# Four-block gated cross-attention kernel: L1's attention in two passes over the batches with split fp32r weights, L3's scores in two halves

## What is computed

```
h   = layernorm(x);   xq = fp8(clip(h / in_scale))      
q, qx = xq @ wq, xq @ wqx  (2 heads a group);  k, v = xq @ wk, xq @ wv  (1 head a group)
kx, vx = ctx @ w_kv_x                                         # in fp32
q, k, qx, kx = layernorm of each head over its 128 features, times weight, plus bias
out = softmax(q k / sqrt(128)) v   and   softmax(qx kx / sqrt(128)) vx      # 4 heads a group in all
x  += gate * proj_scale * (fp8(out / smooth) @ wproj)         # contraction over 2 x 16 heads x 128
```

## Time and profile before

| | us |
|---|---|
| median of 3 runs (2734.95 to 2738.09) | 2735.35 |
| the profiled execution's own time | 2733.31 |
| its span in the trace | 2731.5 |
| L1 attention, 423.6 to 1521 | 1097.4 |
| L3 attention, from its first score at 2462.4 to about 2695 | 233 |

### The profile page before, as it was taken

The page is one execution under the profiler, slowest core; times in us unless marked ns, Lnnn a source line. Parts: engine busy times, 40 slices in busy tenths (PEclk is TensorE's granted clock), DMA queues, the critical chain, the costliest instruction groups (busy, mean ns, idle before and its releaser), DMA issues. The chain is left out here.

```text
span 2731.5 us, 50212 instructions
## 1 busy us (share of the span) xinstructions
PE 2318.3 (85%) x16586; PEld 1983.6 (73%) x16586; DVE 1921.9 (70%) x4961; ACT 1281.8 (47%) x3929; POOL 1194.8 (44%) x2657
## 2 busy tenths in 40 slices
PE   5879991799999999999999599997999994657776
PEld 2368881688888888888888488886888883335555
DVE  5855555688888888888888477776455555975665
ACT  2123321566666666666665233332344442435663
POOL 5800002577777777777777111110344442222222
PEclk9989995999999999999999699998899997768998
DMA  3100004000000000000000300001000000000000
GB/s 130 58 1 1 1 1 187 5 3 3 3 3 3 3 3 3 3 3 4 5 2 1 105 24 24 24 18 47 12 7 7 7 4 0 1 32 28 21 21 32
DMA packets 28880, 57.66 MB, mean 21 GB/s; under 512 B 4816, under 2 KB 22544, under 8 KB 27152
## 3 DMA queue, kind: packets, MB, share of 16 engines
q1 hardware_dynamic: 28624, 54.45, 6.0%
HBM read 52.34 MB, written 2.10 MB: 20 GB/s over the span
## 5 line engine op out<-in xcount | busy, mean ns | idle before, releaser
L1096 PE MATMUL bank<-l_w,l_xq 128*128 128x128 f32 (+1 forms) x2048 | 359.0, 329 | 9.9 <-DVE l_xq L1260 7.1
L1096 PEld LDWEIGHTS bank<-l_w,l_xq 128*128 128x128 f32 x2048 | 300.7, 192 | 31.2 <-DVE l_xq L1260 7.5
L1339 DVE TENSOR_SCALAR xn_T<-xn_T,l_tiny 128x128 f32<-128x128 f32 x768 | 297.1, 453 | 8.4 <-POOL l_tiny L1380 8.3
L1209 ACT ACTIVATE l_qt<-bank,l_head_b,l_head_w 128x256 f32<-128x256 f32 x256 | 144.4, 564 | 288.8 <-PE bank L1141 288.8
L1268 DVE BATCH_NORM_STATS2 l_st<-xn_T 128x6 f32<-128x128 f32 x768 | 212.4, 279 | 13.3 <-ACT l_v L1201 13.0
L788 PE MATMUL bank<-m_xr,m_wgr 128*128 128x512 f32 x864 | 211.1, 394 | 9.2 <-POOL m_wgr L848 9.2
L1388 POOL TENSOR_TENSOR l_pr<-l_pr,l_rowsum 128x512 f32<-128x512 f32 x128 | 134.3, 1049 | 158.5 <-DVE l_rowsum L1334 158.5
L214 POOL TENSOR_TENSOR ln_rstd<-ln_tmp,neg_half 128x16 f32<-128x16 f32 x8 | 23.3, 2910 | 382.0 <-DVE ln_tmp L152 382.0
L788 PEld LDWEIGHTS bank<-m_xr,m_wgr 128*128 128x128 f32 x864 | 159.0, 190 | 39.5 <-issue 9.2
L1183 ACT ACTIVATE l_pr<-bank,l_negmax 128x128 f32<-128x128 f32 x512 | 182.0, 384 | 1.6 <-DVE l_negmax L1347 1.6
L1370 POOL TENSOR_TENSOR l_tiny<-l_tiny,l_consts 128x6 f32<-128x6 f32 x128 | 177.7, 1388 | 10.0
(11 more groups left out here) (318 smaller groups left out, 6267.6 us busy)
## 6 DMA issues: line engine op xcount, KB each, us to landing
l_w<-in_l_w SPq DMA_DIRECT2D x1, 6144.0 KB, 18.1
m_unsplit<-in_m_w SPq DMA_DIRECT2D x14, 384.0 KB, 3.2
m_wg<-in_m_gu SPq DMA_DIRECT2D x18, 256.0 KB, 2.7
l2f_w<-in_l_w SPq DMA_DIRECT2D x3, 1024.0 KB, 6.9
m_wd<-in_m_down SPq DMA_DIRECT2D x18, 128.0 KB, 2.5
x_resident<-in_x SPq DMA_DIRECT2D x4, 512.0 KB, 5.5
l_ctxT<-in_ctxT SPq DMA_DIRECT2D x1, 2048.0 KB, 7.2
l_toep<-in_l_toep SPq DMA_DIRECT2D x16, 128.0 KB, 2.0
```

Of the source, the lines that this page charges most:

```text
L1096: e.matmul(bank[:, to:to + width], XQ[:, v, k, :], W[:, k, g, at:at + width], start=k == 0, stop=k == KT - 1)
L1209: e.activation(tok(QT[:, n % 2, 3 * x:3 * x + 2, :]), ps[:, 0:2 * P], ACT.Identity, bias=head_b[:, 2 * x:2 * x + 1], scale=head_w[:, 2 * x ...
L1339: r = e.tensor_scalar(RAW[:, n % 4, m, :], RAW[:, n % 4, m, :], tiny[:, n % 2, 0, m:m + 1], tiny[:, n % 2, 6, m:m + 1], ALU.subtract, ALU. ...
```

## The change

*L1 attention.* Two passes over the 16 batches, groups 0 to 3 in the first and 4 to 7 in the second: n = 4 q + j, q from 0 to 31, batch q % 16. Weights of only four groups are kept (WR, WXR, WPR), each in two fp32r parts, high and low. They come one group at a time through a room of two slots of 1 MB, which also holds L0's context before; its first two loads are issued when L0's attention ends, the others inside the loop (LOADS). A group is prepared in numbered steps (FILL_PRE, FILL_POST, FILL_OUT): DVE sums each head's weight columns (`fill_means`), POOL subtracts the means in place (`fill_centre`), ACT scales and writes the high part (`fill_high`), DVE and POOL the low parts (`fill_low`, `fill_cross_low`); the output weights likewise on ACT and POOL. Since centred weights give heads whose mean is zero, the norm needs only the sum of squares: ACT squares all six heads in one instruction, DVE reduces them, POOL's statistics have six operations, and DVE's norm is one multiply. Projections are fp32r products with both parts (W) or three of four (context). Exponents lose the accumulator; DVE sums the probabilities (`sum_probs`). The last rounding subtraction of the output goes to POOL. Inputs are scaled on POOL (`affine`), rounded into XS (bf16), stored to HBM in pass one and fetched in pass two, and copied to a doubled XQ by ACT. The residual is added once in each pass. The layernorm ahead no longer counts again.

*L3 attention.* Scores, maxima and exponents go in two halves of four heads; turns and values come one step later; all values of a half batch are one block, two half batches share one bank. DVE makes the fourth copy of turned blocks instead of the first, and adds the result to X itself.

Other hunks only rename semaphores so that stages share them, and lay out the weights by group on the host. The diff, cut to its core:

```diff
@@ project
-                        for k in range(KT):
-                            e.matmul(bank[:, to:to + width], XQ[:, v, k, :], W[:, k, g, at:at + width], start=k == 0, stop=k == KT - 1)
+                        for k in range(KT):
+                            for part in range(2):
+                                e.matmul(bank[:, to:to + width], XQ[:, q % 2, v, k, :], WR[:, j, part, k, at:at + width],
+                                         start=k == 0 and part == 0, stop=k == KT - 1 and part == 1)
                 for k in range(KT):
-                    r = e.matmul(pcross[:, 2 * P:4 * P], CX[:, k, :], WX[:, k, g, :], start=k == 0, stop=k == KT - 1)
+                    for m, (a, c) in enumerate(((0, 0), (0, 1), (1, 0))):
+                        r = e.matmul(pcross[:, 2 * P:4 * P], CXR[:, q % 2, a, k, :], WXR[:, j, c, k, :],
+                                     start=k == 0 and m == 0, stop=k == KT - 1 and m == 2)
@@ tables of the loop
+            FILL_PRE = {0: 0, 1: 1, 2: 5, 3: 7, 4: 62, 5: 63, 6: 71, 7: 72}
+            FILL_POST = {0: 3, 1: 4, 2: 6, 3: 8, 4: 70, 5: 71, 6: 73, 7: 74}
+            FILL_OUT = {0: 9, 1: 10, 2: 11, 3: 12, 4: 76, 5: 77, 6: 78, 7: 79}
+            LOADS = (4, 5, 7, 9, 11, 13, 71, 72, 74, 75)
+            END = N + 18
@@ scalar: raw, square, fills
-                    e.copy(tok(RAW[:, n % 4, 3 * m:3 * m + 3, :]), bank[:, 0:3 * P])
-                    r = e.copy(V[:, n % G, m, :], bank[:, 3 * P:4 * P])
+                    r = e.copy(tok(RAW[:, n % 6, 4 * m:4 * m + 4, :]), bank[:, :])
+            def square(e, n):
+                e.wait_ge(*s_raw(n + 1))
+                if n >= 1:
+                    e.wait_ge(*s_ss(n))
+                e.activation(SQ[:, :, :].rearrange("p (a h) d -> p a h d", a=2), heads(n), ACT.Square).then_inc(s_sq.sem, 1)
+            def fill_high(e, f):
...
+                for v, at, width in SPAN:
+                    for k in range(KT):
+                        e.activation(WR[:, slot, 0, k, at:at + width], W[:, k, at:at + width], ACT.Copy, scale=full_scale[:, v, k:k + 1])
+                e.copy(WXR[:, slot, 0, :, :].rearrange("p k c -> p (k c)"), unsplit(f)[:, 6 * D:8 * D]).then_inc(s_whi.sem, 1)
@@ vector
+                    n = s - 17
+                    if 0 <= n < N and n % J == J - 1:
...
+                    out = 0 <= s - 15 < N
+                    if out:
+                        smooth_out(e, s - 15)
+                    if 0 <= s - 10 < N:
+                        sum_squares(e, s - 10)
+                    if out:
+                        round_out(e, s - 15, 0)
...
+                    summed = sum_probs(e, s - 13) if 0 <= s - 13 < N else None
+                    if out:
+                        round_out(e, s - 15, 1)
+                    if summed:
+                        e.wait_ge(*summed)
+                        e.reciprocal(rowsum[:, (s - 13) % 2, :], rowsum[:, (s - 13) % 2, :]).then_inc(s_inv.sem, 1)
+                    if out:
+                        round_out(e, s - 15, 2)
+                    if s >= 4 and s // J - 1 < B:
+                        quantise_x(e, s // J - 1, s % J)
+                    if out:
+                        round_out(e, s - 15, 3)
+                    if 0 <= s - 11 < N:
+                        norm(e, s - 11)
+                    if 0 <= s - 12 < N:
+                        maximum(e, s - 12)
...
+                    if s in pre:
+                        fill_means(e, pre[s])
+                    if s in post:
+                        fill_low(e, post[s])
+            def norm(e, n):
+                e.wait_ge(*s_rstd(n + 1))
+                rs = tiny[:, n % 2, 3, :].rearrange("p (a h) -> p a h", a=2)
+                e.tensor_tensor(heads(n), heads(n), bc(rs, 3, P), ALU.mult).then_inc(s_norm.sem, 1)
@@ gpsimd
+                    if s in pre:
+                        fill_centre(e, pre[s])
...
+                    n = s - 15
+                    if 0 <= n < N:
+                        e.wait_ge(*s_to(n + 1))
+                        if n >= 2:
+                            e.wait_ge(*s_outp(n - 1))
+                        e.tensor_tensor(tok(CAT[:, n % 2, :, :]), YO[:, n % 2, :], EO[:, :], ALU.subtract).then_inc(s_cat.sem, 1)
                     if 0 <= s - 10 < N:
                         statistics(e, s - 10)
+                    if s % J == 2 and s // J < B:
+                        affine(e, s // J)
...
@@ l3_attention: tensor, scalar, vector
+                    if s < N:
+                        score(e, s, 1)
+                    if 1 <= s <= N:
+                        turn(e, s - 1, 0)
+                        turn(e, s - 1, 1)
+                    if s >= 2:
+                        values(e, s - 2)
+                    if 1 <= s <= N:
+                        turn(e, s - 1, 2)
+                    if s + 1 < N:
+                        score(e, s + 1, 0)
+                    if 1 <= s <= N:
+                        turn(e, s - 1, 3)
...
+                    if s < N:
+                        exponent(e, s, 0)
+                    if s >= 1:
+                        keep_turned(e, s - 1, 0)
+                    if s < N:
+                        exponent(e, s, 1)
+                    if s >= 1:
+                        keep_turned(e, s - 1, 1)
+                        keep_turned(e, s - 1, 2)
...
+                    if s < N:
+                        maximum(e, s, 1)
+                    if s >= 2:
+                        finish(e, s - 2)
+                    if s % 2 == 1 and s // 2 + 2 < B:
+                        normalise(e, s // 2 + 2)
+                    if s + 1 < N:
+                        maximum(e, s + 1, 0)
+                    if 1 <= s <= N:
+                        keep_turned(e, s - 1, 3)
```

More of the change, by code:

```diff
@@ L941, in moe, with l1_staging, load, first @@
             return [acc(N), down(N), high(Q), wds(units)]
-        def l1_attention(ends, loaded, W, WX, scratch):
-            G, NS = 8, 4
+        def l1_staging(scope):
+            room = sb(scope, "l1_stage", [P, 2, 8 * D])
+            order = [("w", 0), ("w", 1), ("w", 2), ("w", 3), ("p", 0), ("p", 1),
+                     ("w", 4), ("w", 5), ("w", 6), ("w", 7), ("p", 2), ("p", 3)]
+            w_in = Slots(signals, "l1_w_loaded", len(order), 16, 2)
+            def load(e, i):
+                kind, f = order[i]
+                e.dma_start(room[:, i % 2, :], A["l1_w" if kind == "w" else "l1_wp"][f]).then_inc(w_in.of(i), 16)
+            def first(e):
+                load(e, 0)
+                load(e, 1)
+            return first, (room, order, w_in, load)
@@ L1161, in tensor @@
                 begin(e, ends)
-                for s in range(G + N + 8):
+                for s in range(END):
                     if 0 <= s - 9 < N:
@@ L1230, in scalar, with fill_out_high @@
+            def fill_out_high(e, f):
+                slot = f % J
+                e.wait_ge(*w_in(at["p", f // 2] + 1))
+                if f >= J:
+                    e.wait_ge(*s_outp(N // 2 - J + slot + 1))
+                e.copy(WPR[:, slot, 0, :, :].rearrange("p h d -> p (h d)"),
+                       unsplit_out(f)).then_inc(s_phi.sem, 1)
             def scalar(e):
                 begin(e, ends)
-                for s in range(G + N + 8):
+                for s in range(END):
                     if 0 <= s - 13 < N:
@@ L1307, in quantise_x, with smooth_out, round_out @@
                     quantised[b] = dve_own.all()
+            def smooth_out(e, n):
+                e.wait_ge(*s_pv(n + 1))
+                if n >= 2:
+                    e.wait_ge(*s_cat(n - 1))
+                e.tensor_tensor(YO[:, n % 2, :].rearrange("p (h t) -> p h t", h=4), pout[:, :].rearrange("p (h t) -> p h t", h=4),
+                                bc(smooth[:, J * (n // (N // 2)) + n % J, :], 2, P), ALU.mult).then_inc(s_smooth.sem, 1)
+            rounded = {}
+            def round_out(e, n, part):
+                e.wait_ge(*(rounded[n] if part else s_smooth(n + 1)))
+                if part == 1 and n >= 1:
+                    e.wait_ge(*s_cat(n))
+                r = round_fp8(e, part, YO[:, n % 2, :], EO[:, :], None)
+                if part == 3:
+                    r.then_inc(s_to.sem, 1)
+                else:
+                    dve_own.did(r)
+                    rounded[n] = dve_own.all()
@@ new lines, in sum_squares, with sum_probs @@
+            def sum_squares(e, n):
+                e.wait_ge(*s_sq(n + 1))
+                if n >= 2:
+                    e.wait_ge(*s_rstd(n - 1))
+                e.tensor_reduce(ssq[:, n % 2, :], SQ[:, :, :], AXX, ALU.add).then_inc(s_ss.sem, 1)
+            def sum_probs(e, n):
+                e.wait_ge(*s_exp(n + 1))
+                if n >= 2:
+                    e.wait_ge(*s_prob(n - 1))
+                dve_own.did(e.tensor_reduce(rowsum[:, n % 2, :], PR[:, n % 2, :, :], AXX, ALU.add))
+                return dve_own.all()
@@ L1350, in statistics @@
             def statistics(e, n):
```

(29 more changed lines are left out.)

715 lines of the change are left out of this document (361 added, 354 removed).

## The result

| | before | after |
|---|---|---|
| median of the runs shown, us | 2735.89 | 2813.3 |
| profiled execution's own time | 2733.31 | 2817.0 |
| its span | 2731.5 | 2815.2 |
| mean granted clock | 0.939 | 0.910 |

A forecast was written before the change was run, and what follows sets the result against it. TensorE led before, DVE close behind; afterwards L1's ring of engines was to bound. Main part -85, setup -8, drain +3, L3 -12 gave -102 us: 2631 on the profiled execution, 2633 as median, range 2565 to 2712.

The forecast's parts named there:

- main part: L1 attention from first to last projection: 64 steps of 7.05, 63 of 6.7, plus 38; 911 us against 996.5.
- the ring: L1 chain of norm, turning, copies, exponents, probabilities' sum, closed once a step: 7.05 us in pass one, 6.7 in pass two.
- Projection: L1's projection as 22 fp32r products, the 128-wide ones starting 0.11 us apart: 2.56 us instead of 3.49.
- rival B: 128-wide fp32r products in L1's projection cost 0.22 us each, PE needs 7.24 a step; total 2699 us; 18%.
- PE's own need: TensorE's time for one L1 step after the change: 6.35 us (5.95 to 7.24), below the ring.
- Rival A: POOL's moved subtraction goes ahead of L1's norm, which waits 1.3 us more each step; total 2798 us; 10%.
- the forecast's sign: L1's norm record would show 0.9 us alone, 1.5 on meeting POOL's multiply, over 2 under rival A.
- Refill: Centring and splitting four weight groups inside L1's loop for pass two: 38 us (20 to 60).
- Setup: Before L1's first projection: 12 us earlier, 4 lost to output weights; -8 us (-20 to +10).
- Drain: End of L1 attention: one step more, partly empty; +3 us (0 to 7).
- L3: L3 attention in halves: step 6.55 us instead of 6.93, 31 times 0.38; -12 us (-40 to +12).

The follow-up runs named there:

- e2: Changed kernel with DVE's last rounding subtraction of the inputs moved from the end to the head of its step: 2721.4 us.
- e6: On e5, DVE norms the heads ahead of the probabilities' sum and POOL does the statistics ahead of the multiply: 2660.7 us.
- e9: On e6, POOL subtracts the refill's means at the end of its step; sums and split of groups 6 and 7 one step later: 2642.0 us.
- e5: On e2, x turned behind the projection, its stream two steps earlier, POOL's input scaling as two operations a step: 2711.6 us.
- e7: Changed kernel with L3's attention as it was before, so L1's change alone: 2823.4 us.
- e10: Changed kernel with e2's edit, and ACT's copy of the rounded inputs to XQ moved to the end of its step: 2822.8 us.

## Why the prediction was wrong

Its main part was 911 us, measured 1095. By steps:

| steps | forecast | after | e2 | e6 | e9 |
|---|---|---|---|---|---|
| 1 to 52 (pass one) | 366.6 | 493.2 | 412.9 | 368.5 | 365.6 |
| 53 to 72 (refill) | 176.2 | 216.2 | 204.4 | 206.4 | 189.2 |
| 73 to 127 (pass two) | 368.5 | 385.7 | 385.9 | 365.5 | 365.1 |
| sum | 911.3 | 1095.2 | 1003.2 | 940.4 | 919.9 |

**The step that failed** is "once in four steps a 1024-wide and a 256-wide copy", put "all at nothing: the ring of 7.05 covers them". I priced `put_xq` as 1 us of ACT's time and did not ask what it waits for, nor what is queued behind it. It waits for the end of DVE's step: 92 us with the clock's fall (e2 against after), half of the 180 between forecast and measurement.

*"POOL ... the input scaling, which takes ACT 3.18 now: 6.0".* I spread ACT's 3.18 us over four steps; on POOL it is one block of 3.6 to 5.1 us, mostly 5.0, in one step's queue. The forecast did not cost x's turning at all, and it makes the 9.2 us step, with POOL's block as the wait behind it; removing both gained 10 us by the medians and 14 in the main part (e5). The trace of the kernel before had both waits, once in eight steps, in steps of 9.16 and 9.2 us where an undisturbed one is 7.28; I took the 7.28 and left the waits out:

```profile
754.15 0.41 PE L1157 MATMUL bank<-ident,l_xn 128*128 128x128 f32 x2 [1.46 <-ACT l_qt L1211]
...
759.72 1.13 PE L1108 MATMUL bank<-l_qt 128*128 128x128 f32 x8 [1.67 <-ACT l_pr L1183]
```

The second was behind ACT's input scaling of 3.19 us, which stood ahead of the exponents.

*Projection.* Right, and rival B is out. Fifty steps of pass two (1191 to 1541 us) by shape, count, busy time and mean ns:

```profile
L1132 PE MATMUL bank<-l_wr,l_xq 128*128 128x256 f32 x400 | 70.4, 297 | 0.0
L1132 PE MATMUL bank<-l_wr,l_xq 128*128 128x128 f32 x400 | 50.1, 268 | 0.0
```

A step's eight narrow products are busy for 1.00 us together, so on average their starts are (1.00 - 0.27) / 7 = 0.105 apart (forecast 0.11, rival B 0.22). The wide ones come in two blocks of four. Inside a block the starts are 0.12 apart, as forecast, but the first one of each block is 0.20 and 0.17 ahead of the second. So the projection as a whole comes out a little longer than the 2.56 us of the sum:

```profile
724.50 2.09 PE L1132 MATMUL bank<-l_wr,l_xq 128*128 128x256 f32 x16
...
727.23 1.13 PE L1146 MATMUL bank<-xn_T 128*128 128x128 f32 x8
```

From its start to the score's it is 2.73 us. PE's own need is then 7.28 - 3.49 + 2.73 = 6.52 us and not 6.35, and the 6.54 of e6 and 6.53 of e9 are that need.

*The ring.* The mechanism was right and shown by e6. Size: 7.01 and 7.34 against 6.7 and 7.05. Pass two once round, after:

```profile
1230.34 1.06 POOL L1544 TENSOR_TENSOR xn_T<-xn_T,l_rowsum 128x512 f32<-128x512 f32 x1 [0.98 <-DVE l_rowsum L1457]
...
1230.54 1.14 DVE L1327 TENSOR_TENSOR l_yo<-l_yo,l_eo 128x512 bf16<-128x512 bf16 x1
...
1231.60 0.94 DVE L1380 TENSOR_TENSOR l_raw<-l_raw,l_tiny 128x768 f32<-128x768 f32 x1
1231.76 1.80 POOL L1551 TENSOR_TENSOR l_cat<-l_yo,l_eo 128x512 fp32r<-128x512 bf16 x1 [0.36 <-DVE l_yo L1327]
...
1232.60 0.88 PE L1179 MATMUL bank<-ident,l_raw 128*128 128x128 f32 x6 [0.26 <-DVE l_raw L1380]
```

The norm (0.94) is not hit; the rounding's add before it is, 1.14 where it takes 0.41 alone: 0.73 against the 0.63 charged to the norm. From the exponents' end (1229.25) to the norm it is 2.35 us, where I had 1.45 plus 0.63. That is the 0.3 of pass two; the 0.29 of pass one was not taken apart.

*Rival A* is out for this kernel: in pass two the norm goes first, and POOL's subtraction pays, 1.80 for 1.15. In pass one 5 of 44 norms (steps 9 to 52) were hit, by the multiply, and took 1.78, where the forecast's sign was 1.5. The price that A named is real, though: in e9 half of pass one's norms (22 of 43) take 1.9, and in this step POOL's subtraction starts 0.11 us ahead of the norm.

```profile
1022.36 1.21 POOL L1557 TENSOR_TENSOR l_cat<-l_yo,l_eo 128x512 fp32r<-128x512 bf16 x1
1022.47 1.92 DVE L1384 TENSOR_TENSOR l_raw<-l_raw,l_tiny 128x768 f32<-128x768 f32 x1
```

*Refill:* 38 (20 to 60) forecast. Without the operations 36 to 44 go, but with the waits the refill costs 64 in e2. *Setup:* -8, of it 12 less to the first projection and 4 more for the output weights; the first projection comes 10.1 us sooner after L0's end, and the first eight steps of the middle, in which the output weights are split, take 69.9 us where eight of 7.05 are 56.4. *Drain:* +3, measured -1.2. *L3:* -12, measured -6.5 in the trace and -10 by e7. Its step, 6.55 in the forecast: it alternates between 6.24 and 6.97, mean 6.60, with PE waiting for DVE's copy and DVE for the value products, as forecast:

```profile
2661.64 0.96 DVE L2274 RECIPROCAL l_rinv<-bank 128x128 f32<-128x128 f32 x1 [1.53 <-PE bank L2206]
...
2665.20 0.68 DVE L2246 COPY l_pt<-bank 128x512 f32<-128x512 f32 x1
...
2666.03 0.63 PE L2189 MATMUL bank<-ident,l_pr 128*128 128x128 f32 x4 [0.57 <-DVE l_pt L2246]
```

e9's main part of 920 us lies near the forecast's 911, but that is luck and does not bear it out. The forecast's limit was the ring, and e6 and e9 have the ring cut: their passes owe 365 us each to a cut that the forecast did not have, and their refill is longer than forecast. With the ring in place and the input copy, the turning and POOL's block mended (e5) the main part is 989 us, 78 above the forecast: 32 in pass one, 28 in the refill and 18 in pass two. No rival had a blocked queue in it.

What stays open: the first eight steps of the middle were not taken apart; nor were the four refill steps of 14 to 18 us that e9 keeps.

## What to carry to other kernels

Cost an operation that comes once in several steps by three questions, not by its length: which operation of which engine releases it, where that one stands in its own queue's step, and what stands behind the waiting one. Where the releaser is the last operation of a step and the waiter is near the head of one, the wait can be most of a step; here PE, left idle for 5.53 us, came back at a granted clock of 0.53. Moving either end can cure it, but the new place must be tested against both neighbours: the copy cost 92 us where its input was late, nothing there with an early input, and 101 at the end of the step, where it was the next projection that was kept waiting.

## What the runs showed of the hardware

*In these rows the port that DVE and POOL share goes to whoever starts first.* With POOL's 512-wide multiply (1.06 us) just begun, DVE's 1024-wide bf16 rounding operation takes 1.26 instead of 0.42. What is left of the multiply is 0.98, and with its own work that would be 1.40, so it waits for nearly all of it:

```profile
728.17 1.06 POOL L1544 TENSOR_TENSOR xn_T<-xn_T,l_rowsum 128x512 f32<-128x512 f32 x1 [2.00 <-DVE l_rowsum L1457]
728.25 1.26 DVE L1321 TENSOR_SCALAR l_yq<-l_yq 128x1024 bf16<-128x1024 bf16 x1
...
979.44 0.42 DVE L1325 TENSOR_SCALAR l_eq<-l_eq 128x1024 bf16<-128x1024 bf16 x1
```

The norm shows both orders: 0.94 when it starts first (POOL 1.80), 1.92 when POOL does (POOL 1.21). The Trainium skill (Trainium Architecture — The Big Picture, What this means for kernel authors) calls the port pair of DVE and GpSimd an exclusive lock, "not a bandwidth split"; these rows agree, to 0.14 us.

*TensorE's clock after a short wait.* I had not expected so little to be followed by a fall, and the same wait was not always followed by one. Behind the twelve waits of 1.46 us for the turning of x (changed kernel, pass one) six projections took 3.66 or 3.76 us, one of them with a granted clock of 0.50 over 2 us, and six took 2.09 to 2.10. In e2 two of twelve were slow. Behind the 29 waits of 2.3 us in e10, 27 projections took 2.6 to 3.8 us. Behind the twelve waits of 5.0 to 5.5 us in pass one every block of value products took 1.8 to 2.1 us instead of 1.03. What decides in the short cases no run here shows.

*fp32r products with a weight load of their own* start about 0.11 us apart at 128 columns and 0.12 at 256, inside a run of the same width: half the columns save next to nothing here.
